# Two narrow attentions on one Trainium2 core: the negated row maxima travel inside the stacked queries

## The reference, cut to what matters

```
x = x + L0_xattn(layernorm(x), ctx, ctx)          # 16 heads of 8, 77 keys
def mla_attention(x):                              # 16 heads of 8, 128 keys, causal
    q = heads(x @ Wq.T)
    latent = layernorm(x @ Wdkv.T, ln_g, ln_b)
    k, v = heads(latent @ Wuk.T), heads(latent @ Wuv.T)
    q, k = apply_rope(q), apply_rope(k)
    scores = einsum('bhqd,bhkd->bhqk', q, k) / sqrt(8)
    attn = softmax(where(causal, scores, -inf), axis=-1)
    return (einsum('bhqk,bhkd->bhqd', attn, v)) @ Wo.T
```

## Time and profile before

| | us |
|---|---|
| median of three runs (least, most) | 1844.98 (1840.79, 1846.32) |
| the profiled execution | 1851.03 |
| its span, first to last instruction | 1849.2 |
| cross attention: first to last negation of maxima (64 batches) | 36.3 to 367.7 |
| self attention: first to last negation | 425.4 to 859.8 |
| a group of four steps, cross attention, in the loop | 21.2 |
| a group of four steps, self attention | 27.1, some up to 30 |

### The profile page before, as it was taken

The page is one execution under the profiler, slowest core; times in us unless marked ns, Lnnn a source line. Parts: engine busy times, 40 slices in busy tenths (PEclk is TensorE's granted clock), DMA queues, the critical chain, the costliest instruction groups (busy, mean ns, idle before and its releaser), DMA issues. The chain is left out here.

```text
span 1849.2 us, 62144 instructions
## 1 busy us (share of the span) xinstructions
PE 1482.8 (80%) x22193; PEld 1106.0 (60%) x22194; DVE 1315.3 (71%) x3697; ACT 1168.7 (63%) x2992; POOL 788.0 (43%) x836
## 2 busy tenths in 40 slices
PE   3999999937899898997335995999999995799990
PEld 2666666615666666665224782677777774677880
DVE  4787888747888888885553664688888885566665
ACT  2676666623555555554324993999999993677770
POOL 1000000022333333330674562447778777766661
PEclk9999999958999999998557996999999997899995
DMA  2222121100100101100012221001111112233228
GB/s 84 62 64 61 57 69 55 33 18 19 37 25 31 37 24 32 37 25 20 30 45 77 75 68 54 25 25 46 45 48 34 36 37 60 83 92 95 74 72 273
DMA packets 119866, 100.82 MB, mean 55 GB/s; under 512 B 18355, under 2 KB 111030, under 8 KB 119632
## 3 DMA queue, kind: packets, MB, share of 16 engines
q1 hardware_dynamic: 97712, 67.62, 12.7%
q0 software_dynamic: 12928, 25.60, 4.0%
q10 hardware_dynamic: 8992, 4.47, 0.8%
HBM read 43.30 MB, written 32.96 MB: 41 GB/s over the span
## 5 line engine op out<-in xcount | busy, mean ns | idle before, releaser
L2656 POOL DMA_INDIRECT e_back<-e_out_rows,e_G x142 | 147.2, 1037 | 77.2 <-issue 51.6
L1611 ACT ACTIVATE w_weights<-w_pS,w_ng 128x77 f32<-128x77 f32 x512 | 158.5, 356 | 21.2 <-DVE w_ng L1708 21.1
L581 ACT ACTIVATE m_PT<-m_pS 128x1024 f32<-128x1024 f32 x128 | 130.5, 1019 | 60.8 <-PE m_pS L451 59.7
L581 ACT ACTIVATE a_PT<-a_pS 77x1024 f32<-77x1024 f32 x128 | 130.5, 1019 | 48.8 <-PE a_pS L451 47.9
L732 DVE TENSOR_REDUCE m_mx<-m_pM 128x8 f32<-128x1024 f32 x128 | 155.3, 1213 | 4.4 <-PE m_pM L422 4.4
L1214 POOL DMA_INDIRECT e_rows<-re_R,re_index x128 | 129.6, 1012 | 55.4 <-issue 48.2
L2677 DVE TENSOR_TENSOR e_gl<-e_g,e_gh 128x512 f16<-128x512 f32 x142 | 98.2, 692 | 58.8 <-ACT e_g L2632 53.4
L852 POOL TENSOR_SCALAR a_var<-a_aggr 128x4 f32<-128x4 f32 x16 | 3.1, 193 | 294.2 <-DVE a_aggr L656 294.2
L1611 ACT ACTIVATION_READ_ACCUMULATOR w_weights<-w_pS,w_ng 128x1 f32 x512 | 121.5, 239 | 0.0
L2629 ACT ACTIVATE e_gh<-e_pU 128x512 f16<-128x512 f32 x142 | 84.8, 597 | 47.6 <-PE e_pU L136 47.6
L134 PE MATMUL e_pL<-YW,e_gh 128*128 x568 | 110.4, 222 | 1.6 <-DVE e_gl L2677 1.3
(11 more groups left out here) (400 smaller groups left out, 5639.7 us busy)
## 6 DMA issues: line engine op xcount, KB each, us to landing
e_G<-e_rows SPq DMA_DIRECT2D x106, 132.0 KB, 2.2
e_B<-e_back SPq DMA_DIRECT2D x16, 512.0 KB, 6.9
X<-in_x SPq DMA_DIRECT2D x16, 256.0 KB, 3.0
Qs<-a_qh SPq DMA_DIRECT2D x128, 32.0 KB
Qs<-m_qh SPq DMA_DIRECT2D x128, 32.0 KB
Ks<-m_kh SPq DMA_DIRECT2D x32, 128.0 KB
YW<-e_back SPq DMA_DIRECT2D x16, 256.0 KB, 3.0
w_stage<-in_late SPq DMA_DIRECT2D x16, 256.0 KB
```

The costliest lines, as they stand in the source:

```text
L581: act.activation(PT[:NK, b % 2, 8 * half:8 * half + 8, :], pS[:NK, :, :], ACT.Exp, scale=float(1.0 / np.sqrt(HD))).then_inc(exp_done, 1)
L1611: ac = act.activation(weights[:, b % 2, n, :], pS[:, n // HB, n % HB, :KC], ACT.Exp, bias=ng[:, b % 2, n:n + 1], scale=-1.0, accum_out=sum ...
L2656: pool.indirect_dma_start(out=back, out_offset=bass.IndirectOffsetOnAxis(ap=G[:, r, s, D:D + 1].bitcast(I32), axis=0), in_=out_rows[:, r, ...
```

## The change

The negated maxima no longer come in by matmuls with `sel`. The fourth row of one head dimension in each half of `Qs` (partitions 3 and 67) takes them by a transfer of 2 x 8 x 128 elements per batch (`send_minus`, on ScalarE's queue), and all fourth rows of `Ks` hold the constant 64 in place of zero. So the maxima must be there before the scores are made: they are computed two batches ahead in place of one, and turned and copied one step earlier. While a buffer's maxima are made, its two rows must hold zero; `stack` clears them first with a transfer from rows that are always zero. The heads are laid out over the partitions so that six transfers in place of twelve stack the queries. In the self attention the slots are turned by one step (k, ks first and q, qs last) and the queries are made two groups ahead; keys are stacked before queries. There VectorE makes `ol` behind the first reduction. In the cross attention `bring` comes behind the stack. The cosine and sine tables are separate for queries and keys. Waits on `sent` are split by queries and keys.

```diff
-            dve.memset(c["Ks"][:].bitcast(F32), 0.0).then_inc(zeroed, 1)
-            dve.memset(c["ng"][:].bitcast(F32), 0.0).then_inc(zeroed, 1)
+            dve.memset(c["Ks"][:].bitcast(F32), SHIFTS).then_inc(zeroed, 1)
...
-            order = ["q", "qs", "k", "ks", "v", "x", "lat", "latT"]
+            order = ["k", "ks", "v", "x", "lat", "latT", "q", "qs"]
...
         def stack(engine, g, p, what):
...
+            if what == "q":
+                engine.dma_start(Qs[3:P:64, p, :, :, :], Qs[7:P:64, p, :, :, :]).then_inc(sent[what], 16)
...
-                    for j in range(HQ):
-                        engine.dma_start(Qs[32 * j + r:32 * j + 32:4, p, :, j % 2, :], (qh, qh, ql)[r][32 * j:32 * j + 32, :]).then_inc(sent, 16)
+                    for e in range(2):
+                        engine.dma_start(Qs[4 * e + r:P:8, p, :, e, :], (qh, qh, ql)[r][64 * e:64 * e + 64, :]).then_inc(sent[what], 16)
...
             def scores(g, p, b, half):
...
+                if half == 0:
+                    minus_here(pe, g, b)
...
-                if half == 0:
-                    pe.wait_ge(mt_kept, lin(g, GB, b + 1))
-                for n in range(HQ):
-                    for o in range(2):
-                        s = slice(64 * o, 64 * o + 64)
-                        mm = pe.matmul(pS[:NK, 4 * o + n, :], c["sel"][s, 4 * half + n, :NK], mT[s, b % 2, :],
-                                       start=False, stop=n == HQ - 1, skip_group_check=True)
...
             def step(g, p, b, nxt, nxt2):
-                gn, pn, bn = (g, p, b + 1) if b < GB - 1 else (shift(g, 1), 1 - p, 0)
+                gn, pn, bn = (g, p, b + 2) if b < GB - 2 else (shift(g, 1), 1 - p, b + 2 - GB)
-                max_transpose(g, p, b)
+                if nxt or b < GB - 1:
+                    max_transpose(*((g, p, b + 1) if b < GB - 1 else (shift(g, 1), 1 - p, 0)))
...
+            def send_minus(g, p, b):
+                act.wait_ge(mt_kept, lin(g, GB, b + 1))
+                settle(act, c)
+                act.dma_start(Qs[3:P:64, p, :, :, b * P:(b + 1) * P], mT[:, b % 2, :]).then_inc(minus_in[b % 2], 16)
...
             def step(g, p, b, nxt, nxt2):
                 one, two = earlier(g, b, 1), earlier(g, b, 2)
+                if nxt or b < GB - 1:
+                    send_minus(*((g, p, b + 1) if b < GB - 1 else (shift(g, 1), 1 - p, 0)))
                 what, gw, far = slot(b, 0, g, nxt, nxt2)
                 if what:
                     part(what, gw)
...
             def keep_max(g, b):
                 dve.wait_ge(mt_ready, lin(g, GB, b + 1))
-                wait(dve, s_ready, lin(g, 2 * GB, 2 * (b - 1)))
-                dve.tensor_copy(mT[:, b % 2, :], pTh[:]).then_inc(mt_kept, 1)
+                minus_here(dve, g, b - 2)
+                settle(dve, c)
+                dve.tensor_copy(mT[:, b % 2, :], pTh[:H]).then_inc(mt_kept, 1)
...
-                if two:
+                if two and not latent:
                     output_lo(*two)
                 if more:
                     take_max(gn, bn, 0)
+                if two and latent:
+                    output_lo(*two)
...
             def group(g, p, nxt, nxt2):
-                if not latent:
-                    bring(g, nxt2)
-                if nxt:
-                    stack(sp, shift(g, 1), 1 - p, "q")
-                    stack(sp, shift(g, 1), 1 - p, "k")
+                if latent:
+                    if nxt:
+                        stack(sp, shift(g, 1), 1 - p, "k")
+                    if nxt2:
+                        stack(sp, shift(g, 2), p, "q")
+                else:
+                    if nxt:
+                        stack(sp, shift(g, 1), 1 - p, "q")
+                        stack(sp, shift(g, 1), 1 - p, "k")
+                    bring(g, nxt2)
```

More of the change, by code:

```diff
@@ L317, in hi_count, with stacked, minus_here @@
         def hi_count(g, what):
-            per = [w for w in order if w in (("x", "qs", "ks", "latT") if latent else ("x", "q", "k"))]
+            per = [w for w in order if w in (("ks", "x", "latT", "qs") if latent else ("x", "q", "k"))]
             if latent and is_first(g):
                 return ["x", "qs", "latT", "ks"].index(what) + 1
-            lead = 2 if latent else 1
-            back = 1 if what in ("x", "latT") else 0
+            lead = 3 if latent else 1
+            back = 1 if what in two_ahead else 0
             return lin(g, len(per), lead + per.index(what) + 1 - back * len(per))
-        def stacked(engine, g):
-            wait(engine, sent, lin(g, 16 * SENT, 0))
+        def stacked(engine, g, what):
+            wait(engine, sent[what], lin(g, 16 * SENT[what], 0))
+        def minus_here(engine, g, b):
+            wait(engine, minus_in[b % 2], lin(g, 16 * GB // 2, 16 * (b // 2 + 1)))
         def stack(engine, g, p, what):
@@ L493, in begin @@
                         maxima(0, 0, 0, (None, 0))
+                    if what == "qs" and k:
+                        maxima(0, 0, 1, (None, 0))
                     project(what, (None, k), k)
@@ L556, in part @@
                     act.wait_ge(used, u + 1)
-                    stacked(act, g)
+                    stacked(act, g, what)
                     act.activation(dst[:, :n], pP[:, :n], ACT.Identity, bias=SM("b" + what)).then_inc(hi_made, 1)
@@ L560, in part @@
                     dst = qh if what == "qs" else kh
-                    stacked(act, g)
+                    stacked(act, g, what[0])
                     act.wait_ge(rope_sum, lin(g, 2, 1 if what == "qs" else 2))
@@ L615, in step @@
                     keep_heads(*one)
-                if latent and b == 1 and nxt2:
+                if latent and b == 0 and nxt2:
                     squares(shift(g, 2))
@@ L787, in begin @@
                         take_max((None, 0), 0, 0)
+                    if what == "qs" and k:
+                        take_max((None, 0), 0, 1)
+                        negate((None, 0), 0)
                     if what == "lat":
@@ L887, in rope @@
                     pool.wait_ge(hi_made, hi_count(g, what))
-                    stacked(pool, g)
+                    stacked(pool, g, what[0])
                     pool.tensor_tensor(lo[:], t1[:, k, :], hi[:], ALU.subtract).then_inc(rope_lo, 1)
@@ L907, in begin @@
                 rope("latT", (None, 1))
+                rows((None, 2))
+                rope("qs", (None, 1))
             def step(g, p, b, nxt, nxt2):
-                if b == 0 and nxt2:
-                    rows(shift(g, 2))
+                if b == GB - 1 and g[1] + 3 < NG:
+                    rows(shift(g, 3))
                 for half_ in (0, 1):
@@ L2815, in shape_constants @@
     ang = i.astype(f)[None, :] * freq[:, None]
-    d = (i % 32) // 4
-    cos, sin = np.cos(ang).astype(f)[d % half], np.sin(ang).astype(f)[d % half]
-    sin = np.where((d < half)[:, None], -sin, sin)
+    turned = {}
+    for what, (_, d) in (("q", q_rows(i)), ("k", k_rows(i))):
+        sin = np.sin(ang).astype(f)[d % half]
+        turned["cos_" + what] = np.cos(ang).astype(f)[d % half]
+        turned["sin_" + what] = np.where((d < half)[:, None], -sin, sin).astype(f)
     across = lambda m: np.ascontiguousarray(np.broadcast_to(m, (P, *m.shape)))
```

117 lines of the change are left out of this document (70 added, 47 removed).

## The result

The changed kernel takes 1873.75 us (median; 1870.51 to 1876.64) where the kernel before takes 1844.15 beside it: a ratio of 1.0162, with a 95% interval from 1.0138 to 1.0185. It is slower by 1.6%. The prediction was 1841 us, with a range from 1812 to 1862: wrong in sign, and outside the range. The profiled execution has a span of 1874.8 us against 1849.2, a difference of 25.6 us. The medians differ by 29.6: the profiled execution of the kernel before lay 6.9 us above its median, that of the changed kernel 2.9.

The account below looks back on a forecast made before the run. VectorE was taken to set the pace in the second attention and end last in the first's query step. Terms -40 + 29 - 3 + 3 + 7 = -4 gave 1847 us profiled, 1841 us on the median, range 1812 to 1862.

Parts of the forecast that it names:

- the queue's hand-overs: First attention: ScalarE waits for mT, then issues the transfer; 0.53 us issue plus 0.15 us of hand-overs, +29 us in all.
- the falls of the clock: First attention's query step: TensorE stands some 1.5 us and its clock falls in 7 of 15 groups, 1 us each, +7.
- the ends: Prologue and last steps of both attentions: more work ahead of the loop, less serial last steps; +3 us, between 0 and +8.
- second attention, steps: Second attention: m_ol behind the first reduction and stacked keys in time shorten the steps; -40 us, bounds -45 and -20.
- the wait of m_ol: Second attention: VectorE's wait for ScalarE's m_oh, 43.2 us in 62 places, expected to be covered by a reduction of 1.21 us.
- What is late next: Second attention, once the waits go: GpSimd's root in the latent step, the cosine product's 0.30 us wait, then VectorE's 6.06 us.
- the missing products: Sixteen selecting matmuls per batch, 1024 in each attention, removed from TensorE; put at nothing in the sum.
- The first rival: First attention: the issue does not hold ScalarE up, costing only the 0.15 us hand-over, and the clock stays; 1813 us, chance 0.25.
- The prediction's own test: First attention: prediction wrong if the transfer's issue stands beside running ScalarE work and its followers don't move.
- the second rival: First attention: the clock falls in every query step and the issue takes 0.67 us; 1858 us, chance 0.25.
- The rival's condition: First attention's query step: the clock falls as soon as TensorE's stand at the output product reaches 1.59 us.
- Two reductions of 1.21 us are the size of it: Prologue and ends of both attentions: the estimate behind +3 us, between 0 and +8.

Follow-up runs that it names:

- e8: Changed kernel, with VectorE making m_ol ahead of the first reduction again in the second attention; 1892.17 us.
- e6: Changed kernel, with GpSimd starting the low halves of keys and queries in the second attention only behind VectorE's two sets of row products; 1863.32 us.
- e2: Changed kernel, with ScalarE waiting for the maxima and issuing their transfer behind a step's first exponential in the first attention; 1813.50 us.
- e7: e2 with sixteen zero products per batch put back at the place of the selecting ones, in both attentions; 1820.88 us.
- e3: Changed kernel, with GpSimd instead of ScalarE issuing the first attention's transfer of the maxima, at the same moment of the step; 1812.35 us.
- e10: e3 with ScalarE issuing one more transfer of the same shape, constant tile to spare tile, at each first-attention step's head, with no new wait; 1813.98 us.
- e12: Changed kernel with the edits of e3 and e6 together; 1803.23 us, ratio to the kernel before 0.9759 to 0.9795.
- e4: Changed kernel, with ScalarE issuing a second transfer of the same maxima into a spare tile right behind the first, in the first attention; 1911.79 us.

## Why the prediction was wrong

The mechanisms of the two main terms were right. What failed is their size and the terms beside them: VectorE's rows taken at their lengths of before (-40, measured -32.8), the queue's hand-overs and the falls of the clock (+32.5, measured +41.1), and the ends (+3, measured +13.2). Its sum against the measured difference of the spans, term by term (63 steps from the first to the last negation, and the ends around them; the prediction rounds the queue to 29 and the sum to -4):

| term | predicted | measured |
|---|---|---|
| second attention, steps | -40 | -32.8 |
| first attention, steps (queue +28.5, clock +7, keys -3) | +32.5 | +41.1 |
| both, ahead of the first and behind the last negation | +3 | +13.2 |
| the rest of the program | 0 | +4.1 |
| sum | -4.5 | +25.6 |

*Second attention.* The mechanism was right: the wait of m_ol went, as did that for the keys, and e8 shows the one to be 20.5 us. The term was mis-sized by 7 us. The sum counted what VectorE no longer waits for, and took its rows at their lengths before; the same edit moved two sets of rows from behind GpSimd's instructions to beside them, +9.9 us, and e6 gets 7.1 of the stage back. "What is late next" named GpSimd's root and not its subtractions. The Trainium skill, "SBUF — State Buffer", section "SBUF: two separate sides", would have warned of it: VectorE, in a mode that uses two ports, or with two inputs in SBUF beside a GpSimd instruction that reads SBUF, and GpSimd share a pair of ports, whichever starts first holds it for its whole instruction, and the other blocks. The row of 0.87 us that ends 0.09 us behind GpSimd's agrees; that VectorE's rows use two ports here, no run shows.

*First attention, the queue.* The place, the issue (0.53 predicted, 0.52 us measured) and the steps that pay were right. Query +1.5 us (predicted 1.37), x +0.5 (0.35), plain +0.2 (0.2): some 34 us in 15, 14 and 16 steps, where 28.5 were predicted. The part that was short is the hand-over, 0.30 us around the issue in the query step where the prediction took 0.15. Beside it lies what the prediction missed: it compared each step with the step before and put the missing products at nothing. The runs show that the new order, with the wait and the issue away from the step's head (e2), makes the first attention 354 us, 16 less than in the profile of before; by the medians the gain of the whole kernel is 5 to 7 us smaller than by the profiles. Fewer products are 7 of it (e7); the other parts, the new rows and the order two batches ahead, are not shown one by one. So the true price of the transfer at the head is 60 to 65 us (e2, e3), the falls of the clock included, of which the prediction saw the half that was a loss against the step before.

*The first rival* gave 1813 us if the issue did not hold ScalarE up. e10 has an issue that doesn't, and takes 1814, but the likeness is luck: the rival has the first attention 8 us longer, in e10 it is 17 shorter. In the changed kernel the issue stands behind a wait, and there it does hold ScalarE up. The prediction's own test, a transfer "beside running ScalarE work", was the right one.

*The clock.* It fell behind the stand in the query step, as the second rival had it, in 13 places, and a fourteenth time into the tail, where the sum let it come in 7. At some 0.4 us a fall in the loop is cheaper than the 1 us or 1.2 us of the sum and the rival, and in the second to fourth groups dearer: an estimated 10 us in the steps where the sum put 7. The rival's condition, a stand of 1.59 us, does not hold, and the length of a stand alone does not tell: in the changed kernel falls follow stands of 1.40 us, and there and in e2 one of 1.47 us in the first group (41.24 to 42.71) is followed by none.

*The ends.* "Two reductions of 1.21 us are the size of it" was the worst term: +13.2 us against +3, and outside its own bounds of 0 to 8. Two batches ahead means that the last two steps of each attention have no maxima to make, and what is left in them is a chain from engine to engine. Behind the last negation the first attention takes 9.0 us longer and the second 3.3; ahead of the first negation it is -1.3 and +2.3. Of the 9.0 us, 3.3 are there in e2 and e3 too (17.2 us against 13.9); the other 5.7 go with the clock, which is at the 1.2 GHz level throughout the changed kernel's tail and at a mean of 0.83 in that of e2. In e6 the same code had 0.78 and took 18.7 us. The tail of e6, then of e2:

```profile
406.00:424.60 18.60, 11.77 (x152) 6.98 (x150) 5.62 (x19) 8.20 (x13) 0.00 (x0) 0.78 0.01 2
```

```profile
348.85:366.06 17.21, 10.30 (x149) 6.47 (x149) 5.60 (x20) 8.19 (x13) 0.00 (x0) 0.83 0.01 3
```

*The sign.* With -40 and +32.5 on the two sides, errors of a fifth and a quarter, both to the same side, were enough to turn it to +8; the ends and the rest made that +25.6. The range allowed for one error at a time.

## What to carry to other kernels

A transfer that ScalarE issued behind a wait cost its whole issue, and the one behind a running instruction cost nothing that could be told: put it where its source has long been ready, or on the queue of an engine that nobody stands behind. A kernel that gains in one stage and loses in another is worth taking apart: here the losing part, moved a few lines, turned a kernel 1.6% slower into one 1.7% faster (e2), and GpSimd's two subtractions moved as well make it 2.2% (e12). When a step is re-ordered, look also at which rows of VectorE now start beside GpSimd's: here they became longer and showed no wait, while GpSimd's kept its 1.16 us. And look at what runs behind the last step, where no other batch covers the chain.

## What the hardware showed that was not expected

- An issue on ScalarE's queue runs beside an activation: 63 more issues of 0.52 us made the attention no longer (352.9 against 355.7 us), while 64 behind a wait made it 36 us longer (e4), part of them by a lower clock.
- A row of VectorE between SBUF tiles that started beside GpSimd's 1.16 us instruction lasted until 0.08 or 0.09 us behind its end, in 13 of 14 groups: 0.87 us in place of 0.27, or 0.60 in place of 0.34. No wait is shown for it; the trace shows a longer row.
- A fall of the granted clock cost little where VectorE and ScalarE set the pace, 0.42 us in a group of 24, and much where only a chain from engine to engine is left: 22.9 us at 0.50 against 17.2 at a mean of 0.83 behind the first attention.
- Filling TensorE's stand with idle products kept the clock at 1.00 in the first groups, but in the loop the fall only moved to other steps, and the group lasted as long.
